# Heads' results scaled, rounded and split in PSUM, and a preference for the TensorE array's present form in the order of work

## The reference, cut to what matters

```
x = x + tanh(g0) * (softmax(q k^T / 8) v) Wo + bo                # 8 heads, keys and values from ctx
q, k, v = y Wq^T + bq, y Wk^T + bk, y Wv^T + bv                  # y = layernorm(x), 16 heads
q = (q / |q| + emb) * softplus(temp)
h = softmax(q k^T / sqrt(32)) v
gates = softmax(h Wr^T + br); keep the 3 largest, times 3        # 15 columns
sw = softmax(h Ws^T + bs); s = 2*sw0*sw0 + 2*sw1*sum(gates)     # shared and routed share, one factor per token
x = x + tanh(g1) * ((h * s) Wp^T + bp)
```

## Time and profile before

| | us |
|---|---|
| median of 3 runs | 4856.84 |
| lowest and highest run | 4849.66, 4885.29 |
| the profiled execution | 4888.63 |
| its span, first to last instruction | 4886.8 |

### The profile page before, as it was taken

How to read it: one execution, slowest core, us unless ns; L and a number is a source line. 1 busy time by engine, 2 the same in 40 slices (tenths; PEclk the granted TensorE clock), 3 DMA queues, 4 the chain that set the end, 5 groups by cost and what they waited for, 6 DMA issues and landing times.

```text
span 4886.8 us, 67578 instructions
## 1 busy us (share of the span) xinstructions
PE 4506.7 (92%) x21568; PEld 2325.8 (48%) x21568; DVE 3069.3 (63%) x3955; ACT 2523.6 (52%) x4577; POOL 3385.7 (69%) x2667
## 2 busy tenths in 40 slices
PE   4699999999999999999899899999998999989985
PEld 3355554555555555555354454544444544435432
DVE  4464646464646464676776767676767767676774
ACT  3253535353535353546556565656556556656562
POOL 1365666676757575667778778687877787877885
PEclk8899999999999999999999999999999999999997
DMA  6456656666666566545344344353534443543522
GB/s 221 111 160 177 177 168 179 179 180 186 160 175 166 159 169 164 157 138 151 91 127 134 83 132 134 89 154 104 139 100 118 130 134 84 145 121 89 154 70 78
DMA packets 516173, 682.50 MB, mean 140 GB/s; under 512 B 42608, under 2 KB 371824, under 8 KB 506608
## 3 DMA queue, kind: packets, MB, share of 16 engines
q1 hardware_dynamic: 515824, 678.18, 49.9%
HBM read 323.83 MB, written 150.99 MB: 97 GB/s over the span
## 4 chain that ended last, share of the span: by engine, by line
PE 76%; issue 7%; DVE 6%; ACT 4%; DMA 3%; POOL 1%; SPq 1%; ACTq 0%; POOLq 0%; DVEq 0%
PE aux L947 26%; PE aux L1039 19%; PE aux L1053 17%; PE aux L1021 7%; PE aux L1065 3%; DVE nm L1378 3%; ACT probs L1237 2%; DVE h_raw L1401 2%; SPq L836 1%; PE aux L991 1%; PE aux L1073 1%; POOL added_f L926 1%; PE aux L967 1%; ACT more L1237 1%; DMA raw<-in_ctxT 1%
## 5 line engine op out<-in xcount | busy, mean ns | idle before, releaser
L926 POOL TENSOR_TENSOR added<-added,probs 128x512 f32<-128x512 f32 x1433 | 1823.6, 1305 | 751.2 <-PE aux L1053 496.7
L1378 DVE TENSOR_REDUCE nm<-aux 128x2 f32<-128x1024 f32 x1536 | 1808.8, 1220 | 842.2 <-PE aux L1021 841.1
L1237 ACT ACTIVATE probs<-aux 128x512 f32<-128x512 f32 x2151 | 1190.9, 597 | 1141.8 <-PE aux L1039 1092.3
L1039 PE MATMUL aux<-stack 128*128 128x512 f32 x4096 | 1409.6, 437 | 103.8 <-ACT probs L1237 50.3
L1039 PEld LDWEIGHTS aux<-stack 128*128 128x128 f32 x4096 | 707.3, 191 | 950.0 <-issue 324.5
L1053 PE MATMUL aux<-probs,v 128*32 128x512 f32 (+1 forms) x4302 | 983.9, 628 | 0.0
L926 POOL TENSOR_TENSOR added_f<-added_f,probs 128x512 f32<-128x512 f32 x537 | 677.4, 1293 | 194.7 <-PE aux L1053 180.6
L947 PE MATMUL aux<-xT_hi,wqk 128*128 128x512 f32 x1536 | 562.0, 415 | 13.5 <-DVE mrow L1393 4.6
L1021 PE MATMUL aux<-ck_hi,cq_hi 32*128 32x512 f32 (+1 forms) x3072 | 460.1, 491 | 112.6 <-DVE nm L1378 90.8
L1021 PEld LDWEIGHTS aux<-ck_hi,cq_hi 32*128 32x128 f32 (+1 forms) x3072 | 182.1, 188 | 549.6 <-issue 529.5
L947 PE MATMUL aux<-wvo,parts 128*128 128x512 f32 x1536 | 409.0, 403 | 35.0 <-issue 35.0
(11 more groups left out here) (129 smaller groups left out, 4355.6 us busy)
## 6 DMA issues: line engine op xcount, KB each, us to landing
wqk<-w_split SPq DMA_DIRECT2D x256, 256.0 KB, 3.7
wvo<-w_split SPq DMA_DIRECT2D x64, 1024.0 KB, 7.3
parts<-h_kept SPq DMA_DIRECT2D x128, 512.0 KB, 4.0
stack<-cq_hi SPq DMA_DIRECT2D x128, 256.0 KB, 5.7
stack<-ck_hi SPq DMA_DIRECT2D x128, 256.0 KB, 6.0
v_kept<-v_out SPq DMA_DIRECT2D x128, 256.0 KB, 2.7
v<-v_kept SPq DMA_DIRECT2D x64, 512.0 KB, 5.3
h_kept<-h_hi SPq DMA_DIRECT2D x128, 256.0 KB, 2.4
```

Of the source, the lines that this page charges most:

```text
L926: pool.tensor_tensor(onto, onto, exp_buffer(T, e), ALU.add).then_inc(added_ok, 1)
L1039: ins = pe.matmul(out, stack[:, g % 2, e * ph.SLOTS + ks, jt * P:(jt + 1) * P], stack[:, g % 2, e * ph.SLOTS + qs, n * HALF:(n + 1) * HALF ...
L1237: act.activation(exp_buffer(T, e), aux[:, o.bank["S", T, e], :], ACT.Exp, scale=ph.SCALE).then_inc(probs_ok, 1)
L1378: dve.tensor_reduce(nm[:, half, first:first + 2 * TT - t:TT], aux[:, b:b + 2, :], axis=AX.X, op=ALU.max, negate=True).then_inc(emptied["dv ...
```

## The change

The scaling by the reciprocal (`ev`) writes back into the PSUM bank `acc` instead of into `h_raw`. The rounding (`hs`) and the subtraction (`hsl`) read that bank. In the self-attention stage the value bias is no longer added to the values but to the heads' results as they are read (the softmax weights sum to 1), by the operations that read the bank; a new ScalarE item `hr` writes `h_raw` with the bias for the gate product, and the low part goes to a new buffer `h_lo`, so that the subtraction waits for the gate product no more. The bank `acc` is emptied by `hsl` instead of `ev`. `bv` is loaded as four columns at the start instead of a broadcast row in the middle. In the planner, `hsl` is no longer in `SHARED` (items that begin only when GpSimd's present one has ended), and `held` is 0.8 in both stages, which adds 0.8 of a step to the wanted step of a TensorE item that would change between tiled and not tiled.

```diff
-AT = (dict(p=[2.5, 15.14, 35.81, 48.12], over=7.63, held=0, ...
-      dict(p=[0.69, 18.6, 36, 50], over=6.09, held=0, ...
+AT = (dict(p=[2.5, 15.14, 35.81, 48.12], over=7.63, held=0.8, ...
+      dict(p=[0.69, 18.6, 36, 50], over=6.09, held=0.8, ...
...
-                self.add(("ev", h), "dve", b + 0.6, [("sma", h), ("PV", T), ("ev", h - 1), ("hw", h - 1)])
+                self.add(("ev", h), "dve", b + 0.6, [("sma", h), ("PV", T), ("ev", h - 1)])
                 if ph.ffn:
-                    self.add(("gt", h), "pe", b + 1, [("ev", h), ("fb", 0)])
+                    self.add(("hr", h), "act", b + 0.9, [("ev", h), ("gt", h - 1)])
+                    self.add(("gt", h), "pe", b + 1, [("hr", h), ("fb", 0)])
...
-                self.add(("hs", h), "act", b + 1, [("ev", h)])
-                self.add(("hsl", h), "dve", b + 1.2, [("hs", h), ("gt", h)])
+                self.add(("hs", h), "act", b + 1, [("ev", h), ("hr", h), ("hw", h - 1)])
+                self.add(("hsl", h), "dve", b + 1.2, [("hs", h)])
...
-    SHARED = ("hsl", "fl")
+    SHARED = ("fl",)
...
-            return [(("ev", unit[1]), banks)]
+            return [(("hsl", unit[1]), banks)]
...
-                        act.activation(h_hi[:], h_raw[:], ACT.Copy).then_inc(h_hi_ok, 1)
+                        if kind == "hr":
...
+                            act.activation(h_raw[:], src, ACT.Identity, bias=bias).then_inc(h_raw_ok, 1)
+                            continue
...
+                        if ffn:
+                            act.activation(h_hi[:], src, ACT.Identity, bias=bias).then_inc(h_hi_ok, 1)
+                        else:
+                            act.activation(h_hi[:], src, ACT.Copy).then_inc(h_hi_ok, 1)
...
-                        dve.tensor_tensor(v_out[:], src, bv[:], ALU.add).then_inc(emptied["dve"], 1)
+                        dve.tensor_copy(v_out[:], src).then_inc(emptied["dve"], 1)
...
+                        whole = aux[:, o.bank["acc", h], :]
                         if ffn:
-
-                            wait_full(dve, ("gt", h))
-                        dve.tensor_tensor(h_raw[:].bitcast(F32R), h_raw[:], h_hi[:].bitcast(F32), ALU.subtract).then_inc(h_lo_ok, 1)
+                            ins = dve.scalar_tensor_tensor(h_lo[:], whole, bv[:, h // 2 % NG:h // 2 % NG + 1], h_hi[:].bitcast(F32), ALU.add, ALU.subtract)
+                        else:
+                            ins = dve.tensor_tensor(h_raw[:].bitcast(F32R), whole, h_hi[:].bitcast(F32), ALU.subtract)
+                        ins.then_inc(emptied["dve"], 1)
...
-                        dve.tensor_tensor(h_raw[:], aux[:, o.bank["acc", h], :], rn[:], ALU.mult).then_inc(emptied["dve"], 1)
+                        whole = aux[:, o.bank["acc", h], :]
+                        dve.tensor_tensor(whole, whole, rn[:], ALU.mult).then_inc(emptied["dve"], 1)
```

More of the change, by code:

```diff
@@ L122 @@
     (NG, ("wl", "pq", "pk", "pqa", "pka", "pql", "pkl", "ss", "ssa", "s2", "s3", "s3p", "sd", "mx", "mxr", "mc", "mt", "ml", "md", "vl")),
-    (TT, ("vp", "vpe", "vs", "ol", "op", "ope", "xb", "st", "xq")), (HALVES, ("sm", "sma", "ev", "acc", "gt", "ga", "hs", "hsl", "hw")),
+    (TT, ("vp", "vpe", "vs", "ol", "op", "ope", "xb", "st", "xq")), (HALVES, ("sm", "sma", "ev", "acc", "gt", "ga", "hr", "hs", "hsl", "hw")),
     (TURN, ("S", "ex", "ad", "PV"))) for kind in kinds}
@@ L539, in attention @@
         xT_lo = sb("xT_lo", [P, NG, N], F32R)
-        qb, sq, qy, more, bv, bo_f, blk, wg, top, glog, gsum, added_f = earlier(
-            ("qb", [P, 2, HALF], F32), ("sq", [P, HALF], F32), ("qy", [P, HALF], F32), ("more", [P, F.NP - X.NP, HALF], F32), ("bv", [P, DM], F32),
+        qb, sq, qy, more, h_lo, bo_f, blk, wg, top, glog, gsum, added_f = earlier(
+            ("qb", [P, 2, HALF], F32), ("sq", [P, HALF], F32), ("qy", [P, HALF], F32), ("more", [P, F.NP - X.NP, HALF], F32), ("h_lo", [P, HALF], F32R),
             ("bo_f", [P, DM], F32), ("blk", [P, P], F32), ("wg", [P, NG, GC], F32), ("top", [P, TT // 2, 8], F32),
@@ L571, in attention @@
         rs = sb("rs", [P, 4, TT])
-        bq, bk = sb("bq", [P, NG]), sb("bk", [P, NG])
+        bq, bk, bv = (sb(name, [P, NG]) for name in ("bq", "bk", "bv"))
         emb, tau, et = sb("emb", [P, NG]), sb("tau", [P, NG]), sb("et", [P, NG])
@@ L727, in _ @@
                             sp.dma_start(bg[:, t, :], small["bg"].partition_broadcast(P)).then_inc(c_in, 16)
-                        for dst, name in ((bq, "bq"), (bk, "bk"), (emb, "emb")):
+                        for dst, name in ((bq, "bq"), (bk, "bk"), (bv, "bv"), (emb, "emb")):
                             sp.dma_start(dst[:], small[name]).then_inc(c_in, 16)
@@ L799, in _ @@
                         j, h = divmod(g, HALVES)
-                        sp.wait_ge(h_lo_ok, g + 1)
+                        wait_emptied(sp, ("acc", g))
                         if j >= 2 and h < 2:
@@ L805, in _ @@
                                 sp.wait_ge(h_loaded[i], 16 * (TT // 2) * (j - 1))
-                        for part, done in enumerate((h_hi[:].bitcast(F32), h_raw[:])):
+                        for part, done in enumerate((h_hi[:].bitcast(F32), h_lo[:].bitcast(F32) if ffn else h_raw[:])):
                             sp.dma_start(h_kept[j % 2, h % 2 * TT // 2:(h % 2 + 1) * TT // 2, :, part, h // 2, :].rearrange("t p c -> p t c"),
@@ L1069, in _ @@
                         out = bank(it)
-                        wait_emptied(pe, ("sm", h))
+                        pe.wait_ge(h_raw_ok, h + 1 - HALVES * B)
                         for t in range(TT // 2):
@@ L1245, in _ @@
                         act.activation(rn[:], rn[:], ACT.Exp, scale=-1.0).then_inc(rinv_ok, 1)
-                    elif kind == "hs":
+                    elif kind in ("hr", "hs"):
                         h = it[1]
+                        src, bias = aux[:, o.bank["acc", h], :], bv[:, h // 2 % NG:h // 2 % NG + 1]
                         wait_emptied(act, ("sm", h))
-                        act.activation(h_hi[:], h_raw[:], ACT.Copy).then_inc(h_hi_ok, 1)
+                        if kind == "hr":
+                            if h > HALVES * B:
+                                wait_full(act, ("gt", h - 1))
+                            else:
+                                act.wait_ge(h_stored, 32 * h)
+                            act.activation(h_raw[:], src, ACT.Identity, bias=bias).then_inc(h_raw_ok, 1)
+                            continue
+                        if h:
+                            act.wait_ge(h_stored, 32 * h)
+                        if ffn:
+                            act.activation(h_hi[:], src, ACT.Identity, bias=bias).then_inc(h_hi_ok, 1)
+                        else:
+                            act.activation(h_hi[:], src, ACT.Copy).then_inc(h_hi_ok, 1)
                     elif kind == "ge":
@@ L1304, in _ @@
                     elif kind == "fb":
-                        dve.wait_ge(f_in, 48)
+                        dve.wait_ge(f_in, 32)
                         link(dve.memset(blk[:], 0.0))
```

18 lines of the change are left out of this document (8 added, 10 removed), and 2 rows, old and new, of the table TAKES.

## The result

The changed kernel takes 5101.79 us (median of 3 runs, 5095.38 to 5114.43) against 4856.84: a ratio of 1.051 (95% interval 1.047 to 1.054). Slower by 245 us, where I had forecast 118 us less.

A forecast was written before the change was run, and what follows sets the result against it. TensorE's own queue was taken as the bound. Results in PSUM (-78) and the preferred form (-40) gave -118 us, from the median 4856.8 to 4739, said as 4740; range 4690 to 4790 at 50%, wider range 4650 to 4885.

The forecast's parts named there:

- What bounds the kernel: TensorE's own queue: its work in the context stage, its work and its stops in the self-attention stage.
- Part 1: Results stay in PSUM: -78 us in all, with bounds at -144 and about +20.
- the removed stops: Self-attention stage: TensorE's stops behind long subtractions go, 71.9 us; with those near the end, -98 us.
- the stops near the end: TensorE's waits of 11.26 us before a gate product and 22.88 before the last output projection; 7.75 and 18 counted as saved.
- my three costs: Self-attention stage: new ScalarE work, a later gate product and the longer-held bank, +10 us each.
- the new work: ScalarE's `hr`, 0.683 us in 64 halves, mostly hidden, taken as +10 us; subtraction 0.744 us instead of 0.69.
- Part 2: TensorE's present array form is preferred in both stages: -40 us, best case -102.
- the unit price: A change of TensorE's form costs 0.10 us entering tiled, 0.09 leaving; a joined block saves about 0.2 us.
- the number: 1 in 5 `PV` was taken to join the one before it: 205 x 0.2 = -40 us.
- the longer-held bank: `acc` stays taken 2 to 4 us longer, 128 times, so maxima products wait: +10 us, bounds 0 to +64.
- Rival 3: Self-attention stage: after paired `PV`, scores wait for exponentials, 256 x 0.71 = +182 us; slower, 4921 us; chance 11%.
- the SBUF part: Results kept in PSUM, so the subtraction no longer has two SBUF inputs: -78 us with its costs.

The follow-up runs named there:

- after: The changed kernel itself, whole change in, against the kernel before: 5101.79 us, ratio 1.051.
- e9: e7 with the self-attention subtraction reading `h_raw` in SBUF instead of the PSUM bank, so two SBUF inputs again: 4879.8 us.
- e2: The changed kernel with `held=0` in both stages: 4838.6 us.
- e10: The kernel before with e7's preference, key dependency and token-load duration, without any of the PSUM edits: 4870.6 us.
- e7: e5 with the planner's duration of the 1 MB token load at 14 us instead of 9.7: 4740.7 us.
- e12: e7 with `held=0` in both stages: 4819.0 us.
- e5: The changed kernel with a self-attention group's first key-projection piece made to follow the last maxima product of the group before: 4792.5 us.
- e1: The kernel before with `held=0.8` in both stages and nothing else: 4988.2 us.
- e4: The changed kernel with `held` 0 in the context stage and 0.8 in the self-attention stage: 5033.1 us.
- e11: e7 with the planner's duration of the output projection's loads at 6 us instead of 4.2: 4719.0 us.
- e3: The changed kernel with `held` 0.8 in the context stage and 0 in the self-attention stage: 4809.7 us.

## Why the prediction was wrong

**What bounds the kernel: right.** TensorE's own queue decides, with its work in the context stage and its stops in the second.

**Part 1, the removed stops: right in mechanism.** In after no subtraction is long, of the stops near the end one of 9.24 us is left, and the reductions no longer stop TensorE for 4 us. e9 shows that two SBUF inputs are the cause of the long subtractions. What they cost in all was not 98 but depends on the order: part 1 alone was worth about 20 us (e2), in the mended order 130 (e10 against e7). In e2 the context batches took 6.6 us more each; with the load's longer duration (e12) they are down from 257.8 to 249.9 us, so this was the late token load just shown, which I had not looked at. And part 1 made the plan itself worse by 40 us (e2's ends at 4702, before's at 4662), where my three costs came to +30. Which of them it was isn't shown. The wait outlasted eight of GpSimd's additions (10.39 us). The Trainium skill (SBUF — State Buffer, section "SBUF: two separate sides") has an exclusive lock for one whole instruction; that one engine waits for the other agrees with the trace, that it waits for one instruction doesn't.

**Part 1, the new work: right where it can be read alone.** 0.687 us for `hr` and 0.751 for the subtraction, against my 0.683 and 0.744.

**Part 2, the unit price: right; the number: too small.** In a context batch 112 changes of form were left of 179, and 7.8 us of busy time went: 0.12 us each, or 0.09 if only the 86 fewer changes between whole and tiled are counted. I had read 0.10 and 0.09 from the earlier trace rows. In sum it brings 78 us in the mended order, where I took 40.

**Two slips that decide nothing.** The long subtractions add up to 168 us, not 171, and the profiled execution before lies 3 us above the range of the runs, not within it.

**The step that failed: that the order stays as good as it was.** I costed the preference by the pairs it makes, and the longer-held bank as a local delay: "It is wanted once per step of some 4.7 us, and other work covers most of that: 0 to 128 x 0.5 = +64." I had named the very item that waits, the maxima product with its four banks, and had the upper end from the mean delay. What I didn't ask is which other items hold banks at that time, and whether they can give them back. Key projections that begin before the last maxima product can't, and the preference lets them begin earlier: against e2's plan the second half of the keys by 2 us in the group of the longer gap, the first half by 17 in that of the shorter. That it does so because they suit the array's full form just then is the likely reason, not shown. In a like batch that costs twice. TensorE's idle time rises from 25 to 52 us, and the clock falls: the time at a granted 0.50, the lower level of 1.2 GHz, rises from 19 to 59 us a batch, in all from 302 to 588. TensorE's busy time rises with it by 13 us a batch; 27 and 13 are the 40 us by which a batch is longer. One dependency that takes this away (e5) is worth 309 us. The term stood at +10 in my sum, with 64 as its bound.

**Rival 3 ended on the right side by the wrong mechanism.** It had scores wait for exponentials. In the second stage their weight loads do wait longer for exponentials of every kind, 365 us instead of 318, but in e5 and e7, which have none of the loss, it is 377 and 388. Its 4921 would have left 181 of the 245 us unexplained.

With the dependency and the load's duration the kernel takes 4741 us, the forecast's number. That is no confirmation of the sum: its terms there are about -35 for the SBUF part without the preference (e12 against before) and -78 for the preference, where I had -78 and -40, and the 35 includes the mending.

**Open.** For e1 the cause is read from its trace, and no run takes it away alone. The batch between the stages takes 288 us in e1 and 292 in after, with a gap of 21 and 22 us before the last maxima product of the second stage's first group; with the dependency it takes 266 (e10) and 269 (e5). After has two inversions a batch and e4 one, though they differ in the context stage's `held` alone; that the state in which the second stage begins decides it is only argued.

## What to carry to other kernels

In a planner that hands out shared buffers in order of need, ask of every item that may begin earlier what it will hold and what must happen before it can give that up; if that is an item which needs the same buffers, write the dependency down, since a good order may avoid the trap only by its offsets. Price a preference by what it lets start early as well as by what it joins. If the planner can be run without the chip, read its own end and its gaps before anything else: here it had 208 of the 245 us. But it knows only the waits in its table. For e1 it said 65 us faster, and the kernel was 125 slower, by subtractions whose length the table doesn't have. After TensorE gets faster, compare the planner's durations of loads with the trace: two of them were too short here, and mending them was worth 52 us (e5 to e7) and, by the context batches of the two traces, 22 (e7 to e11).

## What the runs showed of the hardware

- A VectorE operation with two SBUF inputs beside an unbroken run of GpSimd additions took 10.39 us (e9) and 13.45 us (e1) instead of 0.75; with one input in PSUM the maximum of 64 was 0.753.
- TensorE's granted clock followed its stops: with 19.9 us of idle time in a batch (e7) 6 us of it ran at 0.50, with 52 us (after) 59.
- A 1 MB load took 12.4 us from issue to landing at the most among the other traffic of e3, with a median of 8.5 over sixteen.
